# A decoder's last stage on one Trainium2 core: gate transposes, mixing products and norm statistics put in another order

## The reference

```python
# y is the state-space scan's output over ctx; z, what gates it, is the norm of x
y = y * jax.nn.silu(z)
...
mixed = jnp.einsum('btd,rde->bte', x, factors)
mixed = mixed / math.sqrt(rank) + bias
...
x = x + _L1_attn_ref(_layernorm(x, axis=-1), ...)          # differential attention
x = x + _L1_xattn_ref(ctx_1024, _layernorm(x, axis=-1), ...)  # scan, gated
x = x + _L1_ffn_ref(_layernorm(x, axis=-1), ...)           # mixing by the summed factors
```

## Time and profile before

| what | us |
| --- | --- |
| median of 3 runs (2279.22 to 2287.68) | 2285.29 |
| the profiled execution, its own time | 2284.59 |
| its span, first to last instruction | 2282.8 |
| of it, the last stage from its first DVE instruction (2204.94) to the span's end | 77.9 |

### The profile page before, as it was taken

One profiled execution on the slowest core, in us unless ns is written; L12 is line 12 of the kernel. 1 busy time (PEld: TensorE's weight loads), 2 busy tenths in 40 slices (PEclk: granted clock), 3 DMA queues, 4 the chain that ended last, 5 costly groups with the idle time before them and its releaser, 6 DMA issues. The chain is left out here.

```text
span 2282.8 us, 25533 instructions
## 1 busy us (share of the span) xinstructions
PE 2107.5 (92%) x7606; PEld 1153.2 (51%) x7606; DVE 1759.0 (77%) x3012; ACT 955.2 (42%) x1827; POOL 1063.6 (47%) x810
## 2 busy tenths in 40 slices
PE   6999999999999998998799899999979999999988
PEld 3455455545545553444555646556454544545346
DVE  3888788878887878787888888888856656464777
ACT  2433333324423433664654646547424324232331
POOL 3552443333433441322899899899941101010144
PEclk9999999999999999999999999999989999999999
DMA  7000000000000003445753535525155424232221
GB/s 277 19 24 20 19 19 24 19 19 24 19 21 22 19 15 104 168 179 194 303 187 110 202 125 209 183 92 207 56 180 172 111 77 127 73 111 76 73 88 74
DMA packets 100089, 230.63 MB, mean 101 GB/s; under 512 B 16510, under 2 KB 33792, under 8 KB 97812
## 3 DMA queue, kind: packets, MB, share of 16 engines
q1 hardware_dynamic: 86216, 181.61, 24.0%
q10 hardware_dynamic: 13260, 47.73, 6.0%
q0 software_dynamic: 512, 0.13, 0.0%
HBM read 157.84 MB, written 45.22 MB: 89 GB/s over the span
## 5 line engine op out<-in xcount | busy, mean ns | idle before, releaser
L1619 POOL TENSOR_TENSOR s_state<-s_b_rows,s_delta_u 128x1024 f32<-128x1024 f32 x128 | 303.5, 2384 | 36.8 <-DMA s_b_rows<-scan_bc 34.3
L930 POOL TENSOR_SCALAR a_prob<-a_prob,a_rsum 128x256 f32<-128x256 f32 x256 | 143.2, 579 | 377.6 <-DVE a_rsum L803 377.5
L1662 DVE TENSOR_TENSOR_SCAN s_state<-s_decay,s_state 128x512 f32<-128x512 f32 x256 | 304.5, 1210 | 13.7 <-ACT s_decay L1605 11.2
L1779 PE MATMUL c_bank<-c_xn_parts,c_w_parts 128*128 128x512 f32 (+1 forms) x1056 | 272.9, 409 | 4.2 <-DMA c_w_parts<-ffn_weights_lo 2.6
L1605 ACT ACTIVATE s_decay<-s_delta,s_a 128x512 f32<-128x512 f32 x256 | 173.4, 689 | 226.9 <-DVE s_state L1662 223.3
L455 DVE TENSOR_SCALAR f_picks<-f_mask,f_lut_xor,f_lut 128x260 int32<-128x260 int32 x512 | 229.0, 519 | 7.6 <-DVE f_mask L446 0.9
L1779 PEld LDWEIGHTS c_bank<-c_xn_parts,c_w_parts 128*128 128x128 f32 (+1 forms) x1056 | 198.8, 189 | 65.6 <-issue 14.2
L602 PE MATMUL a_bank<-a_xn_t,a_wq_then_context 128*128 128x512 f32 x512 | 224.3, 592 | 0.0
L663 PE MATMUL a_bank<-a_wo,a_out_t 128*128 128x512 f32 x512 | 222.3, 592 | 0.0
L2345 ACT ACTIVATE d_prob_t<-d_score 128x512 f32<-128x512 f32 x256 | 139.0, 596 | 178.4 <-PE d_score L2196 177.8
L465 DVE COPY_PREDICATED f_picks<-f_mask,f_picks 128x260 int32<-128x260 int32 x448 | 192.9, 489 | 21.2
(11 more groups left out here) (246 smaller groups left out, 3766.3 us busy)
## 6 DMA issues: line engine op xcount, KB each, us to landing
s_b_rows<-scan_bc SPq DMA_DIRECT2D x64, 512.0 KB, 3.7
c_w_parts<-ffn_weights_hi ACTq DMA_DIRECT2D x39, 512.0 KB, 3.6
c_w_parts<-ffn_weights_lo ACTq DMA_DIRECT2D x39, 512.0 KB, 5.1
d_unit<-diff_parts SPq DMA_DIRECT2D x26, 512.0 KB, 3.6
f_idx<-in_idx SPq DMA_DIRECT2D x64, 130.0 KB, 2.2
ffn_weights<-f_picks SPq DMA_DIRECT2D x64, 130.0 KB, 1.8
d_qs<-d_hi SPq DMA_DIRECT2D x128, 64.0 KB, 2.0
r_xn<-in_factors SPq DMA_DIRECT2D x16, 512.0 KB, 3.7
```

The lines of the kernel that those rows point to most:

```text
L1619: pool.tensor_tensor(self.state[:, s], row.broadcast_to([P, 2, T]), self.delta_u[:, h % 2], ALU.mult) \
L1662: dve.tensor_tensor_scan(self.state[:, s, e, :], self.decay[u % 2][:], self.state[:, s, e, :], 0.0, ALU.mult, ALU.add).then_inc(self.scann ...
L1779: mm = nc.tensor.matmul(banks[b][0:width[o], :], w_parts[:, n % SLOTS, w, at:at + width[o]], xn_parts[:, x_, k, :], start=((k, w, x_) == t ...
```

## The change

It does four things.

- The norm statistics of batch 3 for its gate, 4 `bn_stats`, 4 `bn_aggr` and one addition on DVE, leave the last stage. They stand now in the tail of differential attention, between and behind that stage's last additions (`gate_last`, a new `Ahead`); the power on POOL is the first instruction of the last stage on POOL.
- On PE and in the ring, all remaining outputs of batch 0 come ahead of the transposes of batch 1's rows, and those come ahead of the transposes of batch 2's gate.
- On DVE, half of `rows_ahead(2)` goes behind the statistics of batch 1, `rows_last` goes behind the statistics of batch 2, and batch 1's `low_features` and batch 0's last output stand ahead of the addition of batch 2's gate.
- On POOL, half of `multiply(2)` goes behind bias additions, so that three of the four bias additions of batch 0 stand ahead of it.

No arithmetic is added or taken away. The core of the diff:

```diff
@@ -156,10 +156,16 @@
         self.var_ready = core.sem(f"{self.tag}_var_ready")
         self.rstd_ready = core.sem(f"{self.tag}_rstd_ready")
 
+    def tile_stats(self, x, i, *tiles):
+        for tt in tiles:
+            last = self.nc.vector.bn_stats(self.stats[:, tt, :], x[:, i, tt, :])
+        return last
+
     def vector(self, dve, x, i):
-        for tt in range(TT):
-            last = self.nc.vector.bn_stats(self.stats[:, tt, :], x[:, i, tt, :])
-        last.then_inc(self.stats_done, 1)
+        self.tile_stats(x, i, *range(TT)).then_inc(self.stats_done, 1)
+        self.sum_up(dve)
+
+    def sum_up(self, dve):
         dve.wait_ge(self.stats_done, 1)
         for tt in range(TT):
             last = self.nc.vector.bn_aggr(self.mean_var[:, tt, :], self.stats[:, tt, :])
@@ -2515,11 +2521,20 @@
                     mix = ahead["mix_first"]
                     mix.vector(dve, x, 0)
                     add_outputs(i, 2)
+                    for tt in range(3):
+                        b, turn = ring.at(("out", tt), i)
+                        wait_apart(dve, ring.free[b], turn + 1, turned_waited)
+                    last_gate = ahead["gate_last"]
+                    last_gate.tile_stats(x, i, 0, 1, 2)
                     dve.wait_ge(mix.rstd_ready, 1)
                     for row in range(TT):
                         nc.vector.tensor_scalar(rows_kept[:, row, :], x[:, 0, row, :], mix.mean_var[:, row, 0:1],
                                                 mix.rstd[:, row:row + 1], ALU.subtract, ALU.mult)
                     add_outputs(i, 3)
+                    b, turn = ring.at(("out", 3), i)
+                    dve.wait_ge(ring.free[b], turn + 1)
+                    last_gate.tile_stats(x, i, 3).then_inc(last_gate.stats_done, 1)
+                    last_gate.sum_up(dve)
 
             norm_skip(dve, norm, 1)
             dve.sem_inc(norm.xn_ready, TT)
@@ -2608,7 +2623,8 @@
 
     nc = core.nc
     gy = [None] + [sb(f"g_rows_{i}", [P, ET, T], F32) for i in range(1, B)]
-    gate = Norm(core, sb, "g", xn=[gy[B - 1][:, et, :] for et in range(ET)])
+    last_gate = ahead["gate_last"]
+    gate_scaled = core.sem("g_scaled")
     silu_done = core.sem("g_silu")
     gated = core.sem("g_gated")
     gate_xn = core.sem("g_xn")
@@ -2635,8 +2651,8 @@
         return [("out", i, tt) for tt in tiles]
 
     ring = Ring(core.sems("r_full", 8), core.sems("r_free", 8),
-                rows(0) + out(0, 0) + gates(1) + out(0, 1, 2) + gates(2)
-                + rows(1) + out(0, 3) + out(1, 0, 1, 2)
+                rows(0) + out(0, 0) + gates(1) + out(0, 1, 2, 3)
+                + rows(1) + gates(2) + out(1, 0, 1, 2)
                 + rows(2) + out(1, 3) + gates(3) + out(2, 0, 1, 2)
                 + rows(3) + out(2, 3) + out(3, 0, 1, 2, 3))
 
@@ -2696,10 +2712,9 @@
             start_at_one(pe, *ring.free[KD:])
             outputs(0, 0)
             turn_gated(1)
-            outputs(0, 1, 2)
+            outputs(0, 1, 2, 3)
+            turn_rows(1)
             turn_gated(2)
-            turn_rows(1)
-            outputs(0, 3)
             outputs(1, 0, 1, 2)
             turn_rows(2)
             outputs(1, 3)
@@ -2733,8 +2749,8 @@
 
         @block.gpsimd
         def _(pool):
-            def multiply(i):
-                for et in range(ET):
+            def multiply(i, *tiles):
+                for et in tiles:
                     pool.wait_ge(silu_done, (i - 1) * ET + et + 1)
                     nc.gpsimd.tensor_tensor(gy[i][:, et, :], inputs.y(i)[:, et, :], gy[i][:, et, :], ALU.mult) \
                         .then_inc(gated, 1)
@@ -2749,15 +2765,18 @@
             def scale(norm):
                 norm_gpsimd(nc, pool, norm, consts.minus_half, 0)
 
-            multiply(1)
-            multiply(2)
+            nc.gpsimd.tensor_tensor(last_gate.rstd[:], last_gate.var_eps[:], consts.minus_half[:], ALU.pow) \
+                .then_inc(gate_scaled, 1)
+            multiply(1, 0, 1, 2, 3)
+            multiply(2, 0, 1)
             pool.wait_ge(bias_in, 16)
-            scale(gate)
             add_bias(0, 0, 1)
             scale(mix[1])
-            add_bias(0, 2, 3)
+            add_bias(0, 2)
+            multiply(2, 2, 3)
+            add_bias(0, 3)
             scale(mix[2])
-            multiply(3)
+            multiply(3, 0, 1, 2, 3)
             add_bias(1, 0, 1, 2, 3)
             add_bias(2, 0, 1, 2, 3)
             scale(mix[3])
@@ -2772,10 +2791,10 @@
                                             stats.rstd[:, tt:tt + 1], ALU.subtract, ALU.mult).then_inc(gate_xn, 1)
 
             def rows_last():
-                dve.wait_ge(gate.rstd_ready, 1)
+                dve.wait_ge(gate_scaled, 1)
                 for tt in range(TT):
-                    nc.vector.tensor_scalar(gate.xn[tt], x[:, B - 1, tt, :], gate.mean_var[:, tt, 0:1],
-                                            gate.rstd[:, tt:tt + 1], ALU.subtract, ALU.mult).then_inc(gate_xn, 1)
+                    nc.vector.tensor_scalar(gy[B - 1][:, tt, :], x[:, B - 1, tt, :], last_gate.mean_var[:, tt, 0:1],
+                                            last_gate.rstd[:, tt:tt + 1], ALU.subtract, ALU.mult).then_inc(gate_xn, 1)
 
             def low_features(i, *tiles):
                 for k in tiles:
@@ -2809,19 +2828,20 @@
             low_features(0, 1)
             rows_ahead(1, 3)
             low_features(0, 2, 3)
-            rows_ahead(2, 0, 1, 2, 3)
-            norm_stats(nc, dve, gate, x, B - 1, turn=0)
+            rows_ahead(2, 0, 1)
             add_gated(1)
             norm_stats(nc, dve, mix[1], x, 1, turn=0)
+            rows_ahead(2, 2, 3)
             add_outputs(0, 0, 1)
             norm_apply(nc, dve, mix[1], x, 1, turn=0)
             add_outputs(0, 2)
-            rows_last()
+            low_features(1, 0, 1)
+            add_outputs(0, 3)
+            low_features(1, 2, 3)
             add_gated(2)
             norm_stats(nc, dve, mix[2], x, 2, turn=0)
-            low_features(1, 0, 1, 2, 3)
+            rows_last()
             norm_apply(nc, dve, mix[2], x, 2, turn=0)
-            add_outputs(0, 3)
             add_outputs(1, 0, 1, 2)
             low_features(2, 0, 1, 2, 3)
             add_outputs(1, 3)
@@ -2856,7 +2876,7 @@
         sb, _ = keeper(whole)
         x = sb("x_res", [P, B, TT, D], F32)
         consts = Consts(sb)
-        ahead = {name: Ahead(sb, name) for name in ("ffn_first", "diff_first", "mix_first") + GATES_AHEAD}
+        ahead = {name: Ahead(sb, name) for name in ("ffn_first", "diff_first", "mix_first", "gate_last") + GATES_AHEAD}
         with ExitStack() as stage:
             sb, psum = keeper(stage)
             stage_setup(core, sb, dram, x, consts)
```

More of the change, by code:

```diff
@@ L2032, in stage_diff_attention @@
     ones_row = core.sem("d_ones_row")
-    for name in GATES_AHEAD + ("mix_first",):
+    for name in GATES_AHEAD + ("gate_last", "mix_first"):
         ahead[name].taken_in(core)
@@ L2727, in _ @@
                 silu(1, k)
-            silu(2, 0, 1, 2, 3)
+            silu(2, 0, 1)
+            silu(2, 2, 3)
             features(1, 0, 1, 2, 3)
```

## The result

The changed kernel takes 2289.83 us (median of 20 runs, 2283.32 to 2294.71), the one before 2282.25 us (20 runs beside them, 2277.59 to 2289.59). The ratio is 1.0024, with a 95% interval of 1.0014 to 1.0034: slower by some 5.5 us, a quarter of a per cent, so within what was called no change. (The two medians lie 7.6 us apart. Where the text speaks of the timed loss, it means the ratio.) The profiled execution has a span of 2287.4 us, against 2282.8.

A forecast was written before the change was run, and what follows sets the result against it. DVE was taken to bound the last stage until batch 2's rows can be transposed, PE from there. +2.9 - 3.0 + 1.7 = +1.6 us gave 2286.2 us profiled, 2286.9 as median; range 2281.5 to 2291.5.

The forecast's parts named there:

- The start: Tail of differential attention: moved statistics make the last stage start 2.9 us later, bounds 2.6 and 3.3.
- DVE's list to `rows(2)`: Last stage up to batch 2's transposes: DVE's new list takes 40.9 to 41.0 us, against 44.05 before, 3.1 us shorter.
- PE's waits turn into one: Last stage, ahead of batch 2's transposes: PE's removed waits become one of 6 to 7 us, from near 2242.5 to 2248.95.
- The clock: Batch 2's 16 transposes run at PE's lower clock after the long pause: +1.7 us, bounds 0 and 3.4.
- the rival of a shift of the whole program: Whole program: new tiles push every later address and shift the time; chance 0.02 faster, 0.03 slower.
- that the power holds DVE: Last stage: POOL's power delays DVE's scalar operations, +3.3 us in all, 2288.6 us; chance 0.09.
- that the scalar operations miss POOL: Last stage, `norm_apply(1)` and `rows_last`: fewer operations held, sum -0.4 to -3 us, middle 2284.3 us; chance 0.20.
- That the low clock lasts: Last stage, PE after its long pause: lower clock holds for a second spell, +5 us, 2290.3 us; chance 0.14.

The follow-up runs named there:

- order_only: The kernel before with only the last stage's new order, batch 3's statistics left where they were; ratio to the kernel before 1.0012.
- after_again: The changed kernel run again without any edit, for the spread of profiles; ratio to the kernel before 1.0024.
- warm: The changed kernel with 44 idle transposes of the identity on PE ahead of batch 2's row transposes; ratio to the kernel before 1.0006.
- tiles_only: The kernel before with only the new statistics' small tiles allocated, unused, so all later addresses move; ratio to the kernel before 0.9997.
- pad: The changed kernel with 160 unused bytes per partition where the old gate norm's tiles had been in the last stage; ratio to the kernel before 1.0017.
- hold_pool: The changed kernel with POOL waiting for batch 2's normalised rows before batch 3's multiplications; ratio to the kernel before 1.003.
- apply_first: The changed kernel with batch 2's norm applied on DVE ahead of batch 3's gate rows; ratio to the kernel before 1.0012.
- best_held: The changed kernel with statistics spread out, DVE and POOL reordered, unused padding, and batch 1's bias additions held behind batch 3's gate rows; ratio to the kernel before 0.9987.
- stats_only: The kernel before with only batch 3's statistics moved to differential attention, the last stage's order otherwise kept; ratio to the kernel before 0.9996.

## Why the prediction was right, and which term was off

No change, and the range of 2281.5 to 2291.5, held. Part of that is luck. The measured 2289.83 us is already above the forecast's own 2284.5 to 2289, and the forecast was counted from a kernel before at 2285.3 us, while its median in the 20 runs beside was 2282.25. The change itself was forecast at +1.6 us and came out at +3.0 in the profile and some +5.5 in the timed ratio. Of the steps, the start came as told, DVE's list came as told against a starting point that was misread, the gathered wait came in part, and the clock was too small.

- **The start.** +2.76 us, predicted 2.9 with bounds of 2.6 and 3.3. The first three `bn_stats` take 1.88 us, and DVE's later arrival is covered by nothing.
- **DVE's list to `rows(2)`.** From 2209.38 to 2250.35 it takes 40.97 us, predicted 41.0, and the 44.05 us of before that it was set against. Term by term: `norm_apply(1)` 5.08 (4.8), `rows_last` 2.97 (2.8), `norm_apply(2)` 5.71 (5.8). But that DVE sets the pace until `rows(2)` was wrong for the kernel before. DVE's own list was over at 2246.51, after 41.57 us, and from 2239.10 on PE's 36 matmuls were the bound, 9.89 us long with the low clock of 2240 on them. DVE's list got only some 0.6 us shorter, not 3.1, though batch 3's statistics left it: the new places beside POOL took the rest (order_only). The other 2.4 us are the time by which PE had been behind DVE. The sum came out right since it set the new list against PE's old start.
- **PE's waits turn into one.** Half right. Ahead of `rows(2)` it is 5.16 us, where I said 6 to 7. PE's batch 1 products ended at 2245.2, not 2242.5: 1.5 us of that is the stage's later start in this execution, 1.2 is PE's own, with batch 1's transposes at the lower clock (3.21 us). A second wait, 3.31 us ahead of batch 1's rows, is there too. The forecast has DVE's later list for batch 1's rows, but not PE's pause that follows from it.
- **The clock: the term that was mis-sized.** I took 1.7 us, one set of 16 transposes, from a spell of before that ended with its transposes. Here the low level goes on through most of the 12 matmuls: 1.76 + 0.94 us in the chain, less 0.07 for slower products (below), 2.6 us; after_again, where `rows(2)` comes 0.25 us later, has 2.4. warm, which fills the pause, gets 2.06 of it back behind `rows(2)` and 1.55 at the end. order_only shows 2.5 without anything else. It lies between my forecast and its upper bound of 3.4.
- **What no step held.** Slower products, 2.79 us a tile in place of 2.72: 0.22 + 0.38 us in the chain, and 0.07 for the tile of the low spell. The sum had no such term. The only place where the prediction spoke of addresses was the rival of a shift of the whole program. The shift is free (tiles_only), the changed distance is not (pad).

Measured in the profile, +2.76 - 3.08 + 3.29 = +2.97 us, where the forecast had +1.6.

The rivals: that the power holds DVE is refuted. `rows_last` starts with the power of 2241.87, and three of its four are through before it ends. It was instead POOL's power that grew: 1.02 us for `mix_first_rstd`, with no scalar operation on a 128x512 tile beside it, and 1.06, 1.24 and 1.32 us for the three powers beside such operations. By the rule of the Trainium skill (SBUF — State Buffer, Who interferes with whom) whoever issues first has the shared ports for its whole instruction, so the power, once it had them, would have held DVE to its end. The trace disagrees with this for this small operation, beside which two of DVE's start and end; for 128x512 operations it agrees, as hold_pool shows. That the scalar operations miss POOL did not come: both `norm_apply` were held for all four (the first of batch 1's only in part), and `rows_last` for its last. That the low clock lasts came by half: longer than one set of transposes, not two full spells.

One difference stays open. In the profiles the changed part costs 3.0 us, 1.0013 of the whole, and the timed ratio is 1.0024 with a lower end of 1.0014. Some 2.5 us of the 5.5 timed are not located. The profiles' own starts of `mix_first_stats` scatter from 2192.7 to 2203.3 over the twelve profiles. The nine profiles of kernels with statistics of batch 3 in the tail have it at 2199.3 on average, the three of kernels without at 2196.1. With such a scatter that shows nothing, and single profiles can't tell whether 2 us of it belong to the change. For hold_pool it is the same: +2.33 in its way, and a ratio of 1.003.

## What to carry to other kernels

Gathering an engine's short waits into one long one is no gain in itself: here the long pause ended where TensorE became the bound, and the lower clock behind it cost some 2.5 us, while the order brought batch 2's rows no sooner. To say which engine sets the pace up to a point, look whether it has a wait there: PE had none ahead of batch 2's transposes in the kernel before, so it was PE, and not DVE, whose list ended last. When two engines slow each other, cost a moved instruction by its new neighbour on the other engine. And a start that comes sooner is worth only what the engines behind it can follow: hold_pool and apply_first brought `rows(2)` 5 us ahead and gained 0.6 and lost 0.7.

## What was not expected of the hardware

- The same 12 matmuls of 128x512 take 2.72 or 2.80 us at the full clock by where their operands lie relative to each other. 160 bytes per partition of unused tiles decide it.
- POOL's power on 128x4 values takes 1.01 or 1.02 us with none of DVE's 128x512 scalar operations beside it and 1.06 to 1.33 beside them, while it holds none of them.
- After a pause of 5.16 us the lower clock lasted through work of more than 5 us, and after one of only 2.0 us in best_held it came as well, some 1.4 us into the work. After one of 2.43 us in stats_only it did not come, after one of 2.44 us in hold_pool it did. The length of the pause alone doesn't tell.
